# Second attention: each query tile's two maps scaled and added in two column halves; in the last layer, a low part read from PSUM and a norm bias made by pointer scalars

## The chip, the core and the metric

One core of a Trainium2 chip runs the whole program. The metric is device time in microseconds from one execution, the median of three runs. The engines are PE (TensorE, matrix products and transposes), DVE (VectorE), ACT (ScalarE), POOL (GpSimd) and SP (which issues DMAs). Each runs its own list of instructions in order and waits on semaphores that others raise. PE writes only to PSUM, which has eight banks here; POOL can't reach PSUM.

## What is computed

A block of four layers with residuals: attention of 16 heads, a mixture of experts, a second attention that subtracts one softmax map from another, and a gated layer with 4-bit quantization. The change lies in the last two (the shapes for x are 4 x 1024 x 128):

```python
attn = jax.nn.softmax(A1, axis=-1) - lam * jax.nn.softmax(A2, axis=-1)   # 8 heads
O = jnp.einsum('bhqk,bhkd->bhqd', attn, V)
rms = jnp.sqrt(jnp.mean(O * O, axis=-1, keepdims=True) + EPS)
...
x = x + _L1_attn_ref(_layernorm(x), ...)
x = x + _L1_ffn_ref(_layernorm(x), w_gate, w_up, w_down)
# _L1_ffn_ref: q(h) @ q(w_down).T, h = silu(q(x) @ q(w_gate).T) * (q(x) @ q(w_up).T), q = blockwise 4-bit
```

## The kernel before

A planner in plain Python (`plan_all`) writes one list of steps for all engines. Each engine walks through the list and emits its share of each step, so the list sets the order on every engine. `SIGNALS` says how often each step raises which semaphore; `at(name, step, i=k)` is the value after the k-th raise of a step, and `READ` says who frees a PSUM bank.

**The second attention** works on 256 query tiles of 128 rows (`NTAU`; 4 samples, 8 heads, 8 tiles each), one per slot of the loop over `n`. In a slot, per map `s` of the two: PE makes the scores of 128 x 1024 in six matmuls (`score`, L1798); DVE takes the negative row maxima (c_nm, L1376); ACT writes the exponentials and their row sums (`exponent`, L908, into the tile c_P of map s). Then `combine` joins the maps: DVE makes two factors per row (c_rr, L1383 and L1388); POOL multiplies the second map by its factor (L2046) and adds it to the first (L2048). It stands in the slot after the tile's scores. Three slots after the scores PE turns the joined map in two halves of four 128 x 128 blocks (`turn`, L1809); ACT writes a rounded copy (c_DT, L919) and DVE the rest, the low part (`low`, L1401); PE multiplies both with x (`pv`, L1825, into bank 6, copied out as c_Yh on ACT and c_Yl on DVE, L1409) and with the head's folded matrix (`output`, L1835). Every second slot PE makes the next head's left side (`c_project`, L1781), whose low part c_Tl is made on POOL (L2041). Banks 4, 5 and 7 are a ring for turns, outputs and the last layer's products.

**The last layer** is woven in, one pair of token tiles j per 16 slots. `norm1` takes statistics on DVE and a power on POOL (L2073); `norm2` makes the bias -mean/std on DVE (d_nb, L1508), and ACT writes the normed rows. Then come nine small steps of quantization, `xq` and, for the hidden row of the pair before, `hq`: maxima (L1463), scale (L1471), reciprocal (L1473), product (d_tn, L1475), two DVE steps (L1478, L1480), the snaps i = 6 and 7 on POOL (d_tn, L1099), and the product with the scale (L1485, d_x or d_h). `d_turn_x` turns d_x on PE; ACT writes the rounded copy d_xh (L981) and, in full, d_xl_f (L982); `d_turn_low` subtracts (L1514). The place that matters below is where the snaps of `hq` of one pair and `norm2` of the next stand beside two combines. The last query tile (n = 255) has its halves shared between DVE and POOL. The layer norm of the next sample is made in the same loop in three of the stretches.

Of the kernel before, what the change touches and what calls it, by code (L numbers as in the profile page):

```python
# [14 lines left out]
B, T, C = 4, 1024, 128  # L15
# [10 lines left out]
NTAU = B * 64  # L26
# [57 lines left out]
class Tally:  # L84
# [15 lines left out]
    def at(self, name, *step, i=None):  # L100

        return name, self.value[name, step] - (0 if i is None else self.by[name, step] - i)
# [44 lines left out]
def snapped(on_dve):  # L147
# [51 lines left out]
    "c_project_low": {"c_Tl": 1},  # L199
    "score": {"c_S": 1, "c_nm": 1},  # L200
    "exponent": {"c_ex": 1},
    "combine": lambda n: {"c_cc": 2, "c_D": 2, "c_Dd": 2 if n == NTAU - 1 else 0},
    "turn": {"c_tr": 1, "c_dh": 1},
    "low": {"c_dl": 1},
    "pv": lambda p, part: {"c_pv": 1, "c_yh": 1, "c_yl": 1} if part == 3 else {},
# [7 lines left out]
    "turn_weights_low": {"d_wtl": 1},  # L213
    "turn_down": {"d_h_pe": 1, "d_hT": 2},
    "norm1": {"d_ln": 5, "d_lnp": 1},
    "norm2": {"d_ln": 1, "d_xn": 2},
    "xq": lambda j, i: ON_POOL(i),
    "d_turn_x": {"d_x_pe": 1, "d_xh": 2},
    "d_turn_low": {"d_xl": 1},
    "gate": {"d_gu": 1, "d_sg": 1},  # L220
    "gate_factor": {"d_g": 1},
# [40 lines left out]
    "pv": lambda p, part: [("c_yl", "pv", p, 3)],  # L262
    "turn_weights": lambda k: [("d_wth", "turn_weights", k)],
    "turn_down": lambda: [("d_hT", "turn_down")],
    "d_turn_x": lambda j: [("d_xh", "d_turn_x", j)],
    "gate": lambda *a: [("d_g", "gate_factor", *a)],
    "up": lambda *a: [("d_h", "up", *a)],
    "d_turn_h": lambda *a: [("d_hT", "d_turn_h", *a)],
# [260 lines left out]
def memory(nc, io):  # L529

    m = Ctx()
# [13 lines left out]
    def plain(t):  # L545
        name, shape, offset = where[t.name]
        return nc.alloc_sbuf_tensor_at(name + "_f", shape, F32, offset=offset)
# [168 lines left out]
def scalar_engine(e, w, v, m):  # L716
    at, P = v.at, m.P8

    def bank(*step):
        return P[:, v.plan.bank[step], :]  # L720
# [253 lines left out]

    def d_turn_x(j):
        ps = bank("d_turn_x", j)
        hi, full = [t[:, :, :].rearrange("p i q -> p (i q)") for t in (m.fxh, m.fxf)]
        w.wait_ge(*at("d_x_pe", "d_turn_x", j))
        if j:
            w.wait_ge(*at("d_gu", "up", j - 1, 1))  # L980
        e.activation(hi, ps[:, 0:256], ACT.Copy).then_inc(m.S["d_xh"])  # L981
        e.activation(full, ps[:, 0:256], ACT.Copy).then_inc(m.S["d_xh"])  # L982

    def tanh(ps, i):
        e.activation(m.h[:, i, :], ps[:, 0:NF], ACT.Tanh, scale=0.5).then_inc(m.S["d_sg"])
# [20 lines left out]
    def l_gate(i):  # L1006
# [7 lines left out]
                 c_project=c_project, exponent=exponent, turn=turn, pv=pv, output=output, weigh=weigh,  # L1014
                 norm2=norm2, turn_weights=turn_weights,
                 turn_down=turn_down, d_turn_x=d_turn_x, gate=gate, d_turn_h=d_turn_h, l_turn_x=l_turn_x,
                 l_gate=l_gate)
    for kind, *a in v.plan.steps:
# [83 lines left out]
def vector_engine(e, w, v, m):  # L1102
    at, P = v.at, m.P8
# [400 lines left out]
    def norm2(j):  # L1504
        w.wait_ge(*at("d_lnp", "norm1", j))
        if j:
            w.wait_ge(*at("d_xn", "norm2", j - 1))
        e.scalar_tensor_tensor(out=m.fnb[:, :], in0=m.fmv[:, :, 0], scalar=-1.0, in1=m.fvr[:, 1, :], op0=ALU.mult,  # L1508
                               op1=ALU.mult).then_inc(m.S["d_ln"])

    def d_turn_low(j):
        hi, lo, full = [t[:, :, :].rearrange("p i q -> p (i q)") for t in (m.fxh, m.fxl, m.fxf)]
        w.wait_ge(*at("d_xh", "d_turn_x", j))
        e.tensor_tensor(lo, full, hi.bitcast(F32), ALU.subtract).then_inc(m.S["d_xl"])  # L1514

    def double_silu(ps, i):
        e.scalar_tensor_tensor(out=m.h[:, i, :], in0=m.h[:, i, :], scalar=1.0, in1=ps[:, 0:NF], op0=ALU.add,
# [53 lines left out]
    def l_down(i):  # L1571
# [8 lines left out]
                 small_exp=small_exp, scale=scale, fold=fold, c_turn_low=c_turn_low, keep_x=keep_x, score=score,  # L1580
                 combine=combine, low=low, pv=pv, factor=factor, add=add, turn_weights_low=turn_weights_low,
                 norm1=norm1, norm2=norm2, d_turn_low=d_turn_low, gate_factor=gate_factor, up=up, d_down=d_down,
                 l_norm=l_norm, l_turn_x=l_turn_x, l_silu=l_silu, l_times=l_times, l_down=l_down)
    e.memset(m.mh[:, :], -0.5).then_inc(m.S["mh"])
# [7 lines left out]
def tensor_engine(e, w, v, m):  # L1592
    at, P, ident = v.at, m.P8, m.ident

    def bank(*step):

        for t in v.freed(*step):
            w.wait_ge(*t)
        return P[:, v.plan.bank[step], :]
# [201 lines left out]
    def turn(n, half):  # L1801
        ps = bank("turn", n, half)
        if n == NTAU - 1:
            w.wait_ge(*at("c_D" if half else "c_Dd", "combine", n))
        else:
            w.wait_ge(*at("c_D", "combine", n))
        for i in range(4):
            kt = 4 * half + i
            tt = e.transpose(ps[:, 128 * i:128 * i + 128], m.P1[0][n % 4][:, 128 * kt:128 * kt + 128], ident)  # L1809
        tt.then_inc(m.S["c_tr"])  # L1810
# [103 lines left out]
    def l_down(i):  # L1914
# [5 lines left out]
                 divide=divide, turn_o=turn_o, out_project=out_project, m_turn_x=m_turn_x, route=route, spread=spread,  # L1920
                 item=item, down=down, finish=finish, small2=small2, fold=fold, c_turn_x=c_turn_x,
                 c_project=c_project, score=score, turn=turn, pv=pv, output=output, turn_weights=turn_weights,
                 turn_down=turn_down, d_turn_x=d_turn_x, gate=gate, up=up, d_turn_h=d_turn_h, d_down=d_down,
                 l_turn_x=l_turn_x, l_gate=l_gate, l_up=l_up, l_down=l_down)
# [6 lines left out]
def gpsimd_engine(e, w, v, m):  # L1931
    at = v.at
# [108 lines left out]
        e.tensor_tensor(lo, full, hi.bitcast(F32), ALU.subtract).then_inc(m.S["c_Tl"])  # L2041

    def combine(n):
        p0, p1 = [m.P1[s][n % 4][:, T // 2 if n == NTAU - 1 else 0:T] for s in range(2)]
        w.wait_ge(*at("c_cc", "combine", n))
        e.tensor_scalar(p1, p1, m.rr[:, n % 4, 1:2], 0.0, ALU.mult, ALU.add).then_inc(m.S["c_D"])  # L2046
        w.wait_ge(*at("c_D", "combine", n, i=1))
        e.tensor_tensor(p0, p0, p1, ALU.add).then_inc(m.S["c_D"])  # L2048

    def factor(u, first, end):  # L2050
        F, r = m.ff[u % 2], slice(first, end)
# [23 lines left out]
    def l_norm():  # L2075
        for i in range(2):
# [118 lines left out]
def build(nc, io, out):  # L2195
    with ExitStack() as ctx:
        v = Tally(plan_all(), SIGNALS, READ)
        m = memory(nc, io)
        m.P8 = ctx.enter_context(nc.psum_tensor("P", [128, 8, 512], F32))
        names = ["id", "mh", "a_w", "b_w", *[f"x{b}" for b in range(B + 1)], *v.end]  # L2200
        m.S = {n: ctx.enter_context(nc.semaphore(n)) for n in dict.fromkeys(names)}
        block = ctx.enter_context(nc.Block())
        block.sync(lambda e: sync_engine(e, Once(e, m.S), v, m, io, out))
        block.scalar(lambda e: scalar_engine(e, Once(e, m.S), v, m))
        block.vector(lambda e: vector_engine(e, Once(e, m.S), v, m))
        block.gpsimd(lambda e: gpsimd_engine(e, Once(e, m.S), v, m))
        block.tensor(lambda e: tensor_engine(e, Once(e, m.S), v, m))
# [66 lines left out]
```

## Time and profile before

| | us |
|---|---|
| runs | 2936.09, 2948.23, 2939.10 |
| median | 2939.1 |
| the profiled execution, its time | 2946.47 |
| its span, first to last instruction | 2944.7 |
| of it, loop of the second attention and the end | from about 1208 |

The profile is of one execution. A row of a timeline gives the start in us from the span's start, the length in us, engine, line, operation, out<-in, and in brackets the idle time of that engine just before and what ended it. Lengths of one engine overlap a little, since an instruction's end is seen when its result has landed. Windows give each engine's busy time in a stretch.

### The profile page before, as it was taken

To read this page: it belongs to the slowest core of one execution; us is meant where nothing else is said; L and a number is where in the kernel's file an instruction comes from. 1 tells how busy PE (TensorE), PEld (TensorE's weight loads), DVE (VectorE), ACT (ScalarE), POOL (GpSimd) and SP (SyncE) were. 2 spreads that over 40 slices of the span, in tenths; PEclk is the share of its full clock that TensorE was granted. 3 is DMA by queue.
4 is the path that set the end of the run, shared out by engine and by line. 5 is a ranking of instruction groups with operands and counts; after the bars stand their busy time and mean duration, and the time that the engine had idled before them with its cause. 6 is when DMAs were issued, how large, how long until landed. Compare 5 with 4: busy or idle time off the path is not lost.

```text
span 2944.7 us, 46590 instructions
## 1 busy us (share of the span) xinstructions
PE 2752.8 (93%) x16447; PEld 2032.8 (69%) x16447; DVE 2317.6 (79%) x4143; ACT 2126.2 (72%) x4692; POOL 1801.3 (61%) x1357
## 2 busy tenths in 40 slices
PE   6999999999899999999999999999999999999996
PEld 3333333333347777788888888888888888888885
DVE  8888888888937877789788777777777778777876
ACT  2677777777766555677877777777777787777773
POOL 3442524332015555677788777788778787777773
PEclk8899999999989999999999999999999999999997
DMA  1000000000022111000000000000000000000000
GB/s 41 7 7 7 12 7 7 7 7 2 2 76 75 48 48 58 8 1 1 1 1 3 3 1 3 3 1 3 3 1 3 3 1 3 3 1 3 3 3 6
DMA packets 25689, 34.83 MB, mean 12 GB/s; under 512 B 4136, under 2 KB 14952, under 8 KB 25456
## 3 DMA queue, kind: packets, MB, share of 16 engines
q1 hardware_dynamic: 25456, 31.85, 3.4%
q8 instruction: 131, 2.15, 0.3%
q14 instruction: 102, 0.84, 0.1%
HBM read 29.08 MB, written 2.23 MB: 11 GB/s over the span
## 4 chain that ended last, share of the span: by engine, by line
PE 67%; DVE 15%; ACT 8%; issue 6%; POOL 5%; DMA 0%; DVEq 0%; POOLq 0%; ACTq 0%
PE P L1798 18%; PE P L1666 9%; PE P L1825 8%; PE P L1809 6%; PE P L1651 5%; PE P L1727 5%; PE P L1639 4%; ACT a_PT L784 4%; DVE c_nm L1376 4%; DVE c_DT L1401 3%; PE P L1781 3%; PE P L1738 2%; PE P L1835 2%; PE P L1629 2%; POOL d_tn L1099 2%
## 5 line engine op out<-in xcount | busy, mean ns | idle before, releaser
L1376 DVE TENSOR_REDUCE c_nm<-P 128x1 f32<-128x1024 f32 x512 | 624.4, 1220 | 303.9 <-PE P L1798 301.9
L908 ACT ACTIVATE c_P<-P,c_nm 128x1024 f32<-128x1024 f32 x512 | 573.0, 1119 | 251.8 <-DVE c_nm L1376 247.5
L1221 DVE TENSOR_REDUCE a_mx<-P 128x1 f32<-128x512 f32 x1024 | 640.2, 683 | 99.5 <-PE P L1639 95.4
L784 ACT ACTIVATE a_PT<-P 128x512 f32<-128x512 f32 x1024 | 537.1, 603 | 165.4 <-PE P L1651 165.2
L2048 POOL TENSOR_TENSOR c_P<-c_P,c_P 128x1024 f32<-128x1024 f32 (+1 forms) x256 | 623.0, 2434 | 21.3
L2046 POOL TENSOR_SCALAR c_P<-c_P,c_rr 128x1024 f32<-128x1024 f32 (+1 forms) x256 | 300.9, 1176 | 338.4 <-DVE c_rr L1388 338.4
L1825 PE MATMUL P<-c_DT,c_xkh 128*128 128x256 f32 x2048 | 451.7, 283 | 24.7 <-DVE c_Yl L1409 23.0
L1651 PE MATMUL P<-a_Qs,a_Ks 32*128 32x512 f32 x1024 | 344.2, 493 | 59.6 <-ACT a_PT L784 53.2
L1825 PEld LDWEIGHTS P<-c_DT,c_xkh 128*128 128x128 f32 x2048 | 350.2, 189 | 37.0 <-DVE c_Yl L1409 29.2
L1798 PE MATMUL P<-c_xth,c_Th 128*128 128x512 f32 x1024 | 365.1, 437 | 2.8 <-ACT c_P L908 2.8
L1401 DVE TENSOR_TENSOR c_DT<-P,c_DT 128x512 fp32r<-128x512 f32 x512 | 348.4, 681 | 9.0 <-ACT c_DT L919 8.8
L1809 PE MATMUL P<-ident,c_P 128*128 128x128 f32 x2048 | 313.8, 276 | 37.2 <-DVE c_DT L1401 37.1
L1798 PE MATMUL P<-c_xtl,c_Th 128*128 128x512 f32 x1024 | 322.9, 397 | 0.0
L1798 PE MATMUL P<-c_xth,c_Tl 128*128 128x512 f32 x1024 | 319.9, 393 | 0.0
L919 ACT ACTIVATE c_DT<-P 128x512 fp32r<-128x512 f32 x512 | 305.9, 597 | 2.2 <-PE P L1809 1.9
L1639 PEld LDWEIGHTS P<-a_Ks,a_Qs 32*128 32x128 f32 x1024 | 128.6, 190 | 248.6 <-DVE a_mx L1221 193.5
L1639 PE MATMUL P<-a_Ks,a_Qs 32*128 32x512 f32 x1024 | 284.7, 494 | 11.5 <-DVE a_Qs L1213 5.4
L2034 POOL TENSOR_TENSOR b_sg<-b_sg,b_cwB 128x512 f32<-128x512 f32 x128 | 176.3, 1380 | 193.0 <-ACT b_sg L826 192.8
L1825 PE MATMUL P<-c_DT,c_xkl 128*128 128x256 f32 x1024 | 288.2, 281 | 0.0
L1666 PE MATMUL P<-a_PT,a_Vp 128*32 128x512 f32 x2048 | 282.6, 624 | 0.0
L1809 PEld LDWEIGHTS P<-ident,c_P 128*128 128x128 f32 x2048 | 233.3, 140 | 58.8 <-DVE c_DT L1401 58.2
L1651 PEld LDWEIGHTS P<-a_Qs,a_Ks 32*128 32x128 f32 x1024 | 134.7, 187 | 167.4 <-ACT a_PT L784 140.7
(245 smaller groups left out, 5393.6 us busy)
## 6 DMA issues: line engine op xcount, KB each, us to landing
b_cwB<-cw_scratch SPq DMA_DIRECT2D x64, 256.0 KB, 5.0
c_stg<-in_cw SPq DMA_DIRECT2D x8, 640.0 KB, 4.0
a_Qs<-a_mT SPq DMA_DIRECT2D x256, 2.0 KB
b_stg<-in_moe SPq DMA_DIRECT2D x9, 384.0 KB, 3.0
out<-xres SPq DMA_DIRECT2D x15, 128.0 KB, 1.8
xres<-in_x SPq DMA_DIRECT2D x3, 512.0 KB, 7.6
xres<-in_x SPq DMA_DIRECT2D x2, 256.0 KB, 3.0
a_hTl_f<-in_wqk SPq DMA_DIRECT2D x1, 512.0 KB, 3.6
```

The source lines that it names most:

```text
L784: e.activation(m.PT[j][hs % 4][:, :], bank("scores", u, hs, j), ACT.Exp, scale=SCALE).then_inc(m.S["a_exp"])
L908: e.activation(m.P1[s][n % 4][:, :], P[:, k:k + 2, :].rearrange("p c k -> p (c k)"), ACT.Exp, bias=m.nm[:, n % 4, s:s + 1], accum_out=m.sm ...
L1221: e.tensor_reduce(m.mx2[u % 2][:, t // 4, j, t % 4, half:half + 1], bank("maxima", u, t, j, half), AX, ALU.max).then_inc(m.S["a_max_dve"])
L1376: e.tensor_reduce(m.nm[:, n % 4, s:s + 1], P[:, k:k + 2, :].rearrange("p c k -> p (c k)"), AX, ALU.max, negate=True).then_inc(m.S["c_nm"])
L1401: e.tensor_tensor(lo, bank("turn", n, half).rearrange("p (t q) -> p t q", t=4), hi.bitcast(F32), ALU.subtract).then_inc(m.S["c_dl"])
L1639: e.matmul(ps, m.Qs[u % 3][r, 128 * t:128 * t + 128], m.Ks[u % 3][r, 512 * half:512 * half + 512], start=True, stop=True).then_inc(m.S["a_ ...
L1651: e.matmul(ps, m.Ks[u % 3][r, 128 * kt:128 * kt + 128], m.Qs[u % 3][r, 512 * c:512 * c + 512], start=True, stop=True).then_inc(m.S["a_st"])
L1666: tt = e.matmul(O[32 * j:32 * j + 32, :], m.Vp[b % 2][:, at_v:at_v + 32], m.PT[j][hs % 4][:, :], start=(kt == 0), stop=(kt == 7))
L1798: tt = e.matmul(ps[:, c, :], a[:, s, qs], x[:, 512 * c:512 * c + 512], start=(i == 0), stop=(i == 2))
L1809: tt = e.transpose(ps[:, 128 * i:128 * i + 128], m.P1[0][n % 4][:, 128 * kt:128 * kt + 128], ident)
L1825: tt = e.matmul(P[:, 6, 0:256], x[:, 128 * kt:128 * kt + 128], m.DT[p % 2][l][:, kt, :], start=(kt == 0 and j == 0), stop=(kt, j) == (7, 2))
L2048: e.tensor_tensor(p0, p0, p1, ALU.add).then_inc(m.S["c_D"])
```

## The change

1. `combine` on POOL works on columns 0 to 511 and then on 512 to 1023: scale, add, scale, add. It raises c_D four times instead of twice; `turn` of half 0 waits for the second raise, of half 1 for the fourth. The last query tile stays as it was.
2. `d_turn_x` on ACT writes only the rounded copy. `d_turn_low` on DVE subtracts it from the PSUM bank itself, with an added wait on `up` of the pair before, and it is now this step that frees the bank.
3. `norm2` on DVE makes the bias in two instructions of one column each, whose factor is a pointer scalar, in place of one instruction with two tensor inputs.

```diff
-    "combine": lambda n: {"c_cc": 2, "c_D": 2, "c_Dd": 2 if n == NTAU - 1 else 0},
+    "combine": lambda n: {"c_cc": 2, "c_D": 4, "c_Dd": 0} if n < NTAU - 1 else {"c_cc": 2, "c_D": 2, "c_Dd": 2},
...
-    "d_turn_x": lambda j: [("d_xh", "d_turn_x", j)],
+    "d_turn_x": lambda j: [("d_xl", "d_turn_low", j)],
...
         e.activation(hi, ps[:, 0:256], ACT.Copy).then_inc(m.S["d_xh"])
-        e.activation(full, ps[:, 0:256], ACT.Copy).then_inc(m.S["d_xh"])
...
-        e.scalar_tensor_tensor(out=m.fnb[:, :], in0=m.fmv[:, :, 0], scalar=-1.0, in1=m.fvr[:, 1, :], op0=ALU.mult,
-                               op1=ALU.mult).then_inc(m.S["d_ln"])
+        for i in range(2):
+            e.tensor_scalar(m.fnb[:, i:i + 1], m.fmv[:, i, 0:1], m.fvr[:, 1, i:i + 1], -1.0, ALU.mult,
+                            ALU.mult).then_inc(m.S["d_ln"])
...
         w.wait_ge(*at("d_xh", "d_turn_x", j))
-        e.tensor_tensor(lo, full, hi.bitcast(F32), ALU.subtract).then_inc(m.S["d_xl"])
+        if j:
+            w.wait_ge(*at("d_gu", "up", j - 1, 1))
+        e.tensor_tensor(lo, bank("d_turn_x", j)[:, 0:256], hi.bitcast(F32), ALU.subtract).then_inc(m.S["d_xl"])
...
-            w.wait_ge(*at("c_D", "combine", n))
+            w.wait_ge(*at("c_D", "combine", n, i=2 * half + 2))
...
-        p0, p1 = [m.P1[s][n % 4][:, T // 2 if n == NTAU - 1 else 0:T] for s in range(2)]
         w.wait_ge(*at("c_cc", "combine", n))
-        e.tensor_scalar(p1, p1, m.rr[:, n % 4, 1:2], 0.0, ALU.mult, ALU.add).then_inc(m.S["c_D"])
-        w.wait_ge(*at("c_D", "combine", n, i=1))
-        e.tensor_tensor(p0, p0, p1, ALU.add).then_inc(m.S["c_D"])
+        for i, half in enumerate((0, 1) if n < NTAU - 1 else (1,)):
+            p0, p1 = [m.P1[s][n % 4][:, T // 2 * half:T // 2 * half + T // 2] for s in range(2)]
+            e.tensor_scalar(p1, p1, m.rr[:, n % 4, 1:2], 0.0, ALU.mult, ALU.add).then_inc(m.S["c_D"])
+            w.wait_ge(*at("c_D", "combine", n, i=2 * i + 1))
+            e.tensor_tensor(p0, p0, p1, ALU.add).then_inc(m.S["c_D"])
```

How it moves instructions, first on POOL, at the place where two combines stand around the snaps of a hidden row. The operations are the scaling and the sum of c_P, the snaps d_tn, and c_Tl. Before:

```order
L2046 TENSOR_SCALAR c_P_0_184<-c_P_0_184,c_rr 128x1024
L2048 TENSOR_TENSOR c_P_0_180<-c_P_0_180,c_P_0_184 128x1024
L1099 TENSOR_TENSOR d_tn<-d_tn,d_tc 128x704 x2
L2046 TENSOR_SCALAR c_P_1_187<-c_P_1_187,c_rr 128x1024
L2048 TENSOR_TENSOR c_P_1_181<-c_P_1_181,c_P_1_187 128x1024
L2041 TENSOR_TENSOR c_Tl_192<-c_Tl_f,c_Th_191 128x512
```

After:

```order
L2049 TENSOR_SCALAR c_P_0_184<-c_P_0_184,c_rr 128x512
L2051 TENSOR_TENSOR c_P_0_180<-c_P_0_180,c_P_0_184 128x512
L2049 TENSOR_SCALAR c_P_0_184<-c_P_0_184,c_rr 128x512
L2051 TENSOR_TENSOR c_P_0_180<-c_P_0_180,c_P_0_184 128x512
L1098 TENSOR_TENSOR d_tn<-d_tn,d_tc 128x704 x2
L2049 TENSOR_SCALAR c_P_1_187<-c_P_1_187,c_rr 128x512
L2051 TENSOR_TENSOR c_P_1_181<-c_P_1_181,c_P_1_187 128x512
L2049 TENSOR_SCALAR c_P_1_187<-c_P_1_187,c_rr 128x512
L2051 TENSOR_TENSOR c_P_1_181<-c_P_1_181,c_P_1_187 128x512
L2043 TENSOR_TENSOR c_Tl_192<-c_Tl_f,c_Th_191 128x512
```

The two snaps and c_Tl keep their place in the row; ahead of each stand four instructions of 512 columns instead of two of 1024.

On DVE, at the norm of the last layer in the same stretch: the low part of a turned half (c_DT), the bias (d_nb), the row maxima of the next map (c_nm). Before:

```order
L1401 TENSOR_TENSOR c_DT_1_198<-P,c_DT_1_197 128x4x128
L1508 SCALAR_TENSOR_TENSOR d_nb<-d_mv,d_vr 128x2
L1376 TENSOR_REDUCE c_nm<-P 128x1
L1401 TENSOR_TENSOR c_DT_1_198<-P,c_DT_1_197 128x4x128
L1383 RECIPROCAL c_rr<-c_sm_162 128x1
```

After:

```order
L1400 TENSOR_TENSOR c_DT_1_198<-P,c_DT_1_197 128x4x128
L1508 TENSOR_SCALAR d_nb<-d_mv,d_vr 128x1 x2
L1375 TENSOR_REDUCE c_nm<-P 128x1
L1400 TENSOR_TENSOR c_DT_1_198<-P,c_DT_1_197 128x4x128
L1382 RECIPROCAL c_rr<-c_sm_162 128x1
```

The bias stands where it stood, as two instructions in place of one.

## Rows read from the trace of the kernel before

**Rows 1.** The page of the profile: the span, and each engine's busy time.

```profile
span 2944.7 us, 46590 instructions
...
PE 2752.8 (93%) x16447; PEld 2032.8 (69%) x16447; DVE 2317.6 (79%) x4143; ACT 2126.2 (72%) x4692; POOL 1801.3 (61%) x1357
```

**Rows 2.** Two stretches as windows: start:end, length, busy us (instructions), PE clock, DMA.

```profile
1586.00:1693.00 107.00, 101.79 (x640) 90.52 (x639) 82.22 (x136) 81.87 (x196) 82.71 (x55) 1.00 0.01 2
1907.00:2014.00 107.00, 102.03 (x646) 91.01 (x645) 85.27 (x151) 82.71 (x198) 90.87 (x64) 1.00 0.01 2
```

**Rows 3.** Waits of PE from 1210 to 2880 us: total us, times, longest.

```profile
PE P L1809 <- DVE c_DT L1401: 35.3, 98, 1.3
PE P L1825 <- DVE c_Yl L1409: 22.6, 13, 1.8
```

**Rows 4.** Timeline of PE, 1583 to 1616 us: start, length, then the idle time before.

```profile
1590.31 0.38 PE L1781 MATMUL P<-c_xth,c_mh 128*128 128x256 f32 x1 [0.20 <-DVE c_DT L1401]
...
1598.64 0.39 PE L1825 MATMUL P<-c_DT,c_xkh 128*128 128x256 f32 x1 [1.73 <-DVE c_Yl L1409]
...
1603.99 0.65 PE L1809 MATMUL P<-ident,c_P 128*128 128x128 f32 x4 [0.91 <-DVE c_DT L1401]
...
1611.19 0.66 PE L1809 MATMUL P<-ident,c_P 128*128 128x128 f32 x4 [0.35 <-DVE c_DT L1401]
```

**Rows 5.** Timeline of POOL, the same stretch.

```profile
1586.81 1.33 POOL L2046 TENSOR_SCALAR c_P<-c_P,c_rr 128x1024 f32<-128x1024 f32 x1 [1.46 <-DVE c_rr L1388]
1588.23 2.55 POOL L2048 TENSOR_TENSOR c_P<-c_P,c_P 128x1024 f32<-128x1024 f32 x1
1590.74 3.49 POOL L1099 TENSOR_TENSOR d_tn<-d_tn,d_tc 128x704 f32<-128x704 f32 x2
1594.21 1.12 POOL L2046 TENSOR_SCALAR c_P<-c_P,c_rr 128x1024 f32<-128x1024 f32 x1
1595.41 2.88 POOL L2048 TENSOR_TENSOR c_P<-c_P,c_P 128x1024 f32<-128x1024 f32 x1
1598.26 1.28 POOL L2041 TENSOR_TENSOR c_Tl<-c_Tl_f,c_Th 128x512 fp32r<-128x512 f32 x1
...
1603.22 2.38 POOL L2048 TENSOR_TENSOR c_P<-c_P,c_P 128x1024 f32<-128x1024 f32 x1
```

**Rows 6.** Timeline of DVE, the same stretch.

```profile
1587.18 1.34 DVE L1480 TENSOR_SCALAR d_tc<-d_tc 128x704 f32<-128x704 f32 x1
...
1590.17 0.62 DVE L1508 SCALAR_TENSOR_TENSOR d_nb<-d_mv,d_vr 128x2 f32<-128x2 f32 x1
...
1594.36 1.72 DVE L1485 TENSOR_TENSOR d_h<-d_tn,d_sc 128x704 f32<-128x704 f32 x1 [1.06 <-POOL d_tn L1099]
...
1598.50 1.07 DVE L1471 TENSOR_SCALAR d_sc<-d_mx 128x16 f32<-128x16 f32 x1
...
1603.26 0.67 DVE L1401 TENSOR_TENSOR c_DT<-P,c_DT 128x512 fp32r<-128x512 f32 x1
1603.86 2.02 DVE L1475 SCALAR_TENSOR_TENSOR d_tn<-d_x,d_mx 128x256 f32<-128x256 f32 x1
...
1609.31 1.23 DVE L1376 TENSOR_REDUCE c_nm<-P 128x1 f32<-128x1024 f32 x1 [0.67 <-PE P L1798]
```

**Rows 7.** POOL's groups by form: shapes, count, busy us, mean ns.

```profile
L1999 POOL TENSOR_SCALAR a_th<-a_th,a_msk 128x512 f32<-128x512 f32 x61 | 42.1, 691 | 6.0
L2005 POOL TENSOR_TENSOR a_Qs<-a_th,a_tq 128x512 fp32r<-128x512 f32 x31 | 39.5, 1274 | 2.6
```

**Rows 8.** Single lines: count, shortest/median/longest ns, first and last start.

```profile
L1388 DVE TENSOR_SCALAR c_rr<-c_sm,c_nlam,c_rr x256: 271/273/277, 1208.4 to 2892.8; 128x1 f32<-128x1 f32 x128
...
L1409 DVE TENSOR_TENSOR c_Yl<-P,c_Yh x128: 407/424/427, 1235.3 to 2909.8; 128x256 fp32r<-128x256 f32 x128
...
L1514 DVE TENSOR_TENSOR d_xl<-d_xl_f,d_xh x15: 425/490/907, 1411.3 to 2899.4; 128x256 fp32r<-128x256 f32 x15
...
L982 ACT ACTIVATE d_xl_f<-P x15: 378/407/418, 1409.7 to 2898.9; 128x256 f32<-128x256 f32 x15
```

More of the change, by code:

```diff
@@ L215 @@
     "norm1": {"d_ln": 5, "d_lnp": 1},
-    "norm2": {"d_ln": 1, "d_xn": 2},
+    "norm2": {"d_ln": 2, "d_xn": 2},
     "xq": lambda j, i: ON_POOL(i),
-    "d_turn_x": {"d_x_pe": 1, "d_xh": 2},
+    "d_turn_x": {"d_x_pe": 1, "d_xh": 1},
     "d_turn_low": {"d_xl": 1},
@@ L691, in memory @@
     assert top <= c_small, top
-    m.fxf, m.fwf = plain(m.fxl), plain(m.fwl)
+    m.fwf = plain(m.fwl)
     return m
@@ L976, in d_turn_x @@
         ps = bank("d_turn_x", j)
-        hi, full = [t[:, :, :].rearrange("p i q -> p (i q)") for t in (m.fxh, m.fxf)]
+        hi = m.fxh[:, :, :].rearrange("p i q -> p (i q)")
         w.wait_ge(*at("d_x_pe", "d_turn_x", j))
@@ L1507, in norm2 @@
             w.wait_ge(*at("d_xn", "norm2", j - 1))
-        e.scalar_tensor_tensor(out=m.fnb[:, :], in0=m.fmv[:, :, 0], scalar=-1.0, in1=m.fvr[:, 1, :], op0=ALU.mult,
-                               op1=ALU.mult).then_inc(m.S["d_ln"])
+        for i in range(2):
+            e.tensor_scalar(m.fnb[:, i:i + 1], m.fmv[:, i, 0:1], m.fvr[:, 1, i:i + 1], -1.0, ALU.mult,
+                            ALU.mult).then_inc(m.S["d_ln"])
     def d_turn_low(j):
-        hi, lo, full = [t[:, :, :].rearrange("p i q -> p (i q)") for t in (m.fxh, m.fxl, m.fxf)]
+        hi, lo = [t[:, :, :].rearrange("p i q -> p (i q)") for t in (m.fxh, m.fxl)]
         w.wait_ge(*at("d_xh", "d_turn_x", j))
-        e.tensor_tensor(lo, full, hi.bitcast(F32), ALU.subtract).then_inc(m.S["d_xl"])
+        if j:
+            w.wait_ge(*at("d_gu", "up", j - 1, 1))
+        e.tensor_tensor(lo, bank("d_turn_x", j)[:, 0:256], hi.bitcast(F32), ALU.subtract).then_inc(m.S["d_xl"])
     def double_silu(ps, i):
```

## Prediction

> **What bounds the kernel now.** I read the page first, then the windows of the second attention, PE's waits there, and last the timelines of one stretch of 16 query tiles. The page gives a span of 2944.7 us in which PE is busy for 93% and POOL for 61% [rows 1]. The change touches only the second attention and the last layer, which is woven into it. There PE is busy for 101.8 of 107 us at full clock, while DVE, ACT and POOL are all near 82; where the next block's norm is made, POOL reaches 90.9 [rows 2]. So PE is the bound, with about 5 us of gaps in each stretch of 16 tiles. Where are the gaps? In PE's waits all large ones end with DVE: 35.3 us on the low part of the turned map and 22.6 us on c_Yl; no row of PE waits for POOL [rows 3]. So nobody stands at the door of `combine`, the step that is split. Its first sum (POOL, from 1603.22, 2.38 us long) ends at 1605.60, and PE turns this tile at 1611.19, 5.6 us later [rows 4, 5].
>
> The gaps fall at the same place in each stretch: 1.73 us before 1598.64 and 0.91 us before 1603.99, then small ones of 0.2 to 0.5 us [rows 4]. What leads there is seen from POOL and DVE side by side. POOL runs without a gap from 1586.81 to 1599.54: the two instructions of a combine, two snaps of the last layer's hidden row (d_tn, 3.49 us), a second combine, one c_Tl [rows 5]. DVE waits 1.06 us for the second snap, then does d_h (L1485), and all of DVE's work for PE queues behind it: PE starts again 2.56 us after d_h's end [rows 4, 6].
>
> The timelines also show that DVE and POOL stop each other. DVE's d_tn (L1475, 256 columns) starts at 1603.86 and ends at 1605.88, 0.28 us after POOL's sum; DVE's d_h starts at 1594.36, in POOL's scaling, which ends at 1595.33, and ends 0.75 us after that, at 1596.08; the POOL sum that was issued at 1595.41 takes 2.88 us instead of 2.38, as it waits for d_h; L1471, on 16 columns, starts at 1598.50 and ends at 1599.57, when POOL's c_Tl ends [rows 5, 6]. So a DVE instruction of that kind waits for the end of the POOL instruction in progress, and goes before POOL's next one. This is the mechanism by which shorter POOL instructions can help.
>
> **The split of the combine.** Removed per tile: one scaling and one sum over 1024 columns, undisturbed 1.12 and 2.38 us, with 0.08 us between them [rows 5]; in all 3.58 us. Added: two pairs over 512 columns. The nearest rows are a scaling with a pointer scalar, 0.69 us, and a sum, 1.27 us [rows 7]. The tile then takes 2 x (0.69 + 0.08 + 1.27) = 4.08 us, 0.50 more, on 255 tiles. The last tile is as before. Bounds for the extra: 0 (work scales with columns) and 0.9 (each half sum costs 0.2 more than that row); I take 0.5. On the whole POOL has room: 16 x 0.5 = 8 us more makes 91 of 107, and 99 in the three fullest stretches [rows 2]. The first half of a map is ready 1.5 us earlier (after 2.04 instead of 3.58 us), which pays nothing, since PE comes 5.6 us later. The c_Tl behind it comes later too; the scores that need it start at about the gap of 1603.99, 4.4 us after its end at 1599.54 [rows 4, 5]. Cover: both.
>
> What counts is the piece of POOL's queue ahead of the second snap. **First half of the place.** Now the scaling is issued at 1586.81, takes 1.33 us, and DVE's L1480 waits for it until 1588.52 [rows 5, 6]. With halves: scaling done at about 1587.72 (0.69 plus the same 0.21 of delay); L1480 then needs 0.4 and ends at 1588.14, 0.38 earlier; the sum waits for it and ends at 1589.4; second scaling to 1590.1; second sum to 1591.4; two snaps of together 3.49 end at 1594.85 instead of 1594.23. So the second snap is 0.6 late. **Second half.** Call the end of the second snap S. Now d_h must wait for the scaling of 1.12 and ends at S + 1.85. With halves it waits for 0.69 and ends at S' + 1.44, with S' = S + 0.62: S + 2.06, so 0.2 late. PE's gap of 1.73 becomes 1.9. Then: first sum to S' + 2.65, second scaling to S' + 3.35, second sum from S' + 3.43 to S' + 4.70. L1471 starts 2.42 us after d_h's end [rows 6], at S' + 3.86, inside this second sum, and ends with it: S' + 4.73 = S + 5.35. Now it ends at 1599.57 = S + 5.34. So DVE is again where it was, and DVE is what PE waits for at 1603.99: the low part at 1603.26 [rows 4, 6]. The longer first gap is given back in the second. Sum for this place: 0.0 us, with 0.4 us of doubt on either side (POOL's extra per pair between 0 and 0.9, two pairs on the way), times 14 stretches (15 tile pairs go through the last layer inside the loop, and the first finds no hidden row of an earlier one there): 0 ± 11 us, taken as 12.
>
> **Third place**, d_tn and the two L1478/L1480 behind it. Now d_tn loses 1.5 us to the sum, and the two after it none, because POOL does a c_ff then. With halves d_tn ends at 1604.3 instead of 1605.88; but the other two each meet a new POOL half, and I get 1606.6 for their end instead of 1606.5. DVE has 0.67 us to spare before 1609.31 [rows 6], so either way PE sees nothing: 0.
>
> **The norm's bias.** One instruction on 128x2 with two tensor inputs, 0.62 us, which ends with POOL's sum (1588.23 + 2.55 = 1590.78) [rows 5, 6], goes; two with a pointer scalar on 128x1 come, 0.27 us each in a row of that form that never varied (271 to 277 ns in 256) [rows 8]. They cost some 0.45 us together, at most 0.54. Gain 0.1 to 0.2 us on DVE, but DVE waits 1.06 us for the snap right behind [rows 6], so it is worth 0. If both waited for POOL the cost would be 0.
>
> **The low part from PSUM.** Removed: 15 ACT copies of 0.41 us. The subtraction now reads PSUM; such a one took 407 to 427 ns in 128 cases, where the old one took 425 to 907 [rows 8]. DVE gains 0.07 (median) to 0.5 us each; neither is where PE's gaps are made. The added wait on `up` of the tile pair before is long past. The bank goes free with DVE's read instead of ACT's second one; the ring of three banks comes back to it only with the third take after it. Worth 0; if the cover fails, 0.4 us x 15 = 6.
>
> On that last row a rule of the Trainium skill bears (GPSIMD Engine Reference, Specifications): GpSimd's SBUF interface is shared with VectorE, and collisions come with DVE instructions that have two SBUF inputs or use two ports. By that rule the subtraction from PSUM never waits for POOL, and DVE gains 15 x 0.15 = 2 us on the mean by it; by the old row's 0.49 it would gain 1 us. The trace agrees so far: all 128 c_Yl are undisturbed.
>
> **Sum.** Period place 0, third place 0, bias 0, low part 0; for the end of the loop, where PE waits for DVE almost all the time and the snaps come late once more, +1 us. On the profiled execution 2946.5 + 1 = 2947.5. That execution lies 7.4 us above the median of 2939.1; on the median I forecast **2940 us**.
>
> **Rivals.** *Gain:* the locks shrink more than POOL grows. This holds if a half costs POOL less than rows 7 say, so that L1471 no longer waits: 1.07 x 14 = 15 us [rows 6], 2925. For it: DVE's waits for POOL are real and long. Against: behind the combine stands c_Tl, the next POOL instruction to wait for. *Loss:* L1471 comes after the second sum's end and so waits for c_Tl, another 1.28 us [rows 5], and PE's second gap grows by it: 14 x 1.28 = 18 us, 2958. It decides at 0.84 us (S' + 4.70 against S' + 3.86); one d_h that is delayed by one more half instruction does it. *Not what it says:* somebody waits for the first half after all, and the split frees him; no row shows one, so it would be the forecast's time.
>
> **Chances.** Forecast, with its ± 12: 0.80, of which a little at either rim. Gain 0.09, loss 0.11. A measurement of this kernel tells about 0.5% (14.7 us) from no change, so faster 0.09, same 0.80, slower 0.11. The range is the forecast's own, 2928 to 2952.
>
> **What would show it.** Right: L2048's successors at 1.27 us and L2046's at 0.69; the second snap 0.6 us later after the norm's bias; d_h (L1485) near 1.3 instead of 1.72 us; PE's gap before the pv matmul near 1.9 and the next one near 0.7. Wrong: PE waiting for POOL in a turn, an L1471 that ends with c_Tl, or stretches of 16 tiles that are no longer 107 us long. If halves cost 1.6 us each, as they would if DVE disturbed every one, POOL fills the three full stretches and the sum is off.

## The result and the profile after

The changed kernel took 2956.8 us (median of 20 runs) against 2948.1 us for the kernel before beside it (20 runs): ratio 1.004, with a 95% interval of 1.0028 to 1.0052. The medians lie 8.7 us apart, and the ratio, taken over all runs, is worth 12 us. The change is thus 9 to 12 us slower: inside what was called "no change" (0.5%), but clear of zero, and 2956.8 lies above the predicted range. The page of the changed kernel, and the two windows of [rows 2]:

```profile
span 2950.7 us, 47341 instructions
...
PE 2754.4 (93%) x16447; PEld 2038.9 (69%) x16447; DVE 2292.1 (78%) x4158; ACT 2123.8 (72%) x4677; POOL 1906.6 (65%) x1867
```

```profile
1586.00:1693.00 107.00, 101.40 (x637) 90.14 (x635) 80.43 (x135) 80.92 (x194) 88.62 (x87) 1.00 0.01 2
1907.00:2014.00 107.00, 101.12 (x643) 90.64 (x643) 83.61 (x154) 82.75 (x197) 96.08 (x96) 1.00 0.01 2
```

Against [rows 1, 2], POOL has 105 us more work, 5 to 6 us in each 107, DVE has 25 us less, and PE's busy time over the whole span is nearly the same. In the 14 stretches of 16 tiles (from the first d_nb to the last, first before, then after) it isn't:

```profile
1379.53:2873.89 1494.36, 1431.92 (x8975) 1277.44 (x8975) 1152.36 (x1939) 1145.93 (x2731) 1177.15 (x796) 1.00 0.01 2
```

```profile
1373.77:2878.15 1504.38, 1438.65 (x8975) 1284.31 (x8975) 1132.72 (x1953) 1143.14 (x2717) 1269.45 (x1245) 0.99 0.01 2
```

For the same 8975 instructions PE is busy for 6.7 us more, and it is idle for 3.3 us more (65.7 against 62.4). The place with the snaps looks as the prediction drew it. POOL, start and length:

```profile
1582.27 0.89 POOL L2049 TENSOR_SCALAR c_P<-c_P,c_rr 128x512 f32<-128x512 f32 x1 [1.39 <-DVE c_rr L1387]
1583.25 1.44 POOL L2051 TENSOR_TENSOR c_P<-c_P,c_P 128x512 f32<-128x512 f32 x1
1584.66 0.69 POOL L2049 TENSOR_SCALAR c_P<-c_P,c_rr 128x512 f32<-128x512 f32 x1
1585.44 1.29 POOL L2051 TENSOR_TENSOR c_P<-c_P,c_P 128x512 f32<-128x512 f32 x1
1586.68 3.50 POOL L1098 TENSOR_TENSOR d_tn<-d_tn,d_tc 128x704 f32<-128x704 f32 x2
1590.16 0.69 POOL L2049 TENSOR_SCALAR c_P<-c_P,c_rr 128x512 f32<-128x512 f32 x1
```

The snaps end 7.91 us after the first scaling began, and 7.42 us in [rows 5]: 0.49 us late. DVE in the same stretch:

```profile
1582.64 0.91 DVE L1479 TENSOR_SCALAR d_tc<-d_tc 128x704 f32<-128x704 f32 x1
...
1585.19 0.32 DVE L1508 TENSOR_SCALAR d_nb<-d_mv,d_vr 128x1 f32<-128x1 f32 x2
...
1590.31 1.28 DVE L1484 TENSOR_TENSOR d_h<-d_tn,d_sc 128x704 f32<-128x704 f32 x1 [2.04 <-POOL d_tn L1098]
...
1594.01 0.76 DVE L1470 TENSOR_SCALAR d_sc<-d_mx 128x16 f32<-128x16 f32 x1
```

The product d_h takes 1.28 us instead of 1.72, and the scale d_sc 0.76 instead of 1.07 [rows 6], but DVE waits 2.04 us for the snap instead of 1.06. PE's waits from 1210 to 2880 us (total, times, longest), to be laid beside [rows 3]; the first block is of the kernel before, rows that were not shown there:

```profile
PE P L1781 <- DVE c_DT L1401: 3.1, 15, 0.3
PE P L1825 <- DVE c_xkl L1368: 1.7, 3, 0.6
```

```profile
PE P L1811 <- DVE c_DT L1400: 29.9, 97, 1.1
PE P L1827 <- DVE c_Yl L1408: 29.1, 13, 2.2
PE P L1783 <- DVE c_DT L1400: 4.5, 13, 0.7
...
PE P L1827 <- DVE c_xkl L1367: 3.2, 3, 1.1
```

The wait ahead of the pv matmul for c_Yl rose from 22.6 to 29.1 us, the one of the turns for the low part fell from 35.3 to 29.9. So part of the second gap of the place moved into the first: 1.73 and 0.91 us before [rows 4], 2.23 and 0.67 after. Behind the longer one this is seen on PE (timeline, start and length; first at one place, then 110 us later):

```profile
1484.73 0.58 PE L1827 MATMUL P<-c_DT,c_xkh 128*128 128x256 f32 x1 [2.25 <-DVE c_Yl L1408]
1485.11 0.42 PE L1827 MATMUL P<-c_DT,c_xkl 128*128 128x256 f32 x1
...
1594.15 0.38 PE L1827 MATMUL P<-c_DT,c_xkh 128*128 128x256 f32 x1 [2.23 <-DVE c_Yl L1408]
1594.38 0.28 PE L1827 MATMUL P<-c_DT,c_xkl 128*128 128x256 f32 x1
...
1599.20 0.66 PE L1811 MATMUL P<-ident,c_P 128*128 128x128 f32 x4 [0.67 <-DVE c_DT L1400]
```

The same matmuls, the same gap ahead of them, and 0.42 us instead of 0.28 for one. Windows of PE's granted clock (last but two column) ahead of the first place and in it:

```profile
1477.00:1481.50 4.50, 4.50 (x31) 4.15 (x31) 2.25 (x7) 4.09 (x11) 4.35 (x4) 1.00 0.00 0
1484.50:1487.50 3.00, 2.77 (x12) 2.67 (x13) 2.93 (x7) 1.73 (x4) 2.05 (x2) 0.50 0.00 0
```

PE was busy at full clock, then idle for 2.25 us, and came back at a granted clock of 0.50, the 1.2 GHz level. I call this a fall. In the 14 stretches of 16 tiles inside the loop there are 2 falls in the kernel before and 7 in the changed one. What one costs is read from neighbouring stretches (from one d_nb to the next): before, 107.1 us with a fall and 106.1 without; after, 107.6 and 106.4. So about 1.1 us (0.7 to 1.2 in these two kernels). All these are plain stretches, without a layer norm and without c_xkl; most others are up to 2 us longer in either kernel. Two sums result. Five falls more are some 5.5 us. And a stretch without a fall is 0.3 us longer (106.4 against 106.1), 4 us in 14. From the first combine to the end the traces differ by 12.1 us (1748.1 against 1736.0), as much as the ratio says: 10.0 us in the 14 stretches, 2 us outside them, most of it behind the last. (The spans differ by 6.0 only, since the profiled execution of after happened to be 6 us shorter ahead of the first combine, where nothing is changed.)

### The profile page after: what moved, and what is told of

Same layout as the page of the kernel before. It is cut to its first block, busy times and chain, and to the rows that moved or that the text cites. A ratio compares the mean times of both kernels' runs of the same rounds, so it can differ in the third digit from the quotient of the medians.

```text
span 2950.7 us, 47341 instructions
## 1 busy us (share of the span) xinstructions
PE 2754.4 (93%) x16447; PEld 2038.9 (69%) x16447; DVE 2292.1 (78%) x4158; ACT 2123.8 (72%) x4677; POOL 1906.6 (65%) x1867
## 3 DMA queue, kind: packets, MB, share of 16 engines
HBM read 29.08 MB, written 2.23 MB: 11 GB/s over the span
## 4 chain that ended last, share of the span: by engine, by line
PE 73%; DVE 14%; ACT 7%; issue 5%; POOL 2%; DMA 0%; DVEq 0%; POOLq 0%
PE P L1800 21%; PE P L1827 9%; PE P L1668 8%; PE P L1811 7%; PE P L1653 5%; PE P L1729 5%; PE P L1641 4%; DVE c_nm L1375 4%; ACT a_PT L784 4%; DVE c_DT L1400 3%; PE P L1783 3%; PE P L1837 2%; PE P L1740 2%; PE P L1631 2%; DVE a_mx L1220 1%
## 5 line engine op out<-in xcount | busy, mean ns | idle before, releaser
L2051 POOL TENSOR_TENSOR c_P<-c_P,c_P 128x512 f32<-128x512 f32 x511 | 668.8, 1309 | 42.6
L2049 POOL TENSOR_SCALAR c_P<-c_P,c_rr 128x512 f32<-128x512 f32 x511 | 370.7, 725 | 224.3 <-DVE c_rr L1387 224.2
```

## The experiments

I began with two theories. **Clock (C):** the split lengthens one gap of PE, and the clock behind it is the cost. **POOL (P):** each halved tile costs by its additional 0.5 us of POOL work, wherever it stands. A third (O), that the two small edits cost something, went with the first two runs. In all of them the reference is the kernel before, run beside them.

**One part alone, and the whole without it.** The first is the kernel before with edit 1 only (its lines with +), the second the changed kernel with edit 1 taken back (with -):

```diff
+        for i, half in enumerate((0, 1) if n < NTAU - 1 else (1,)):
+            p0, p1 = [m.P1[s][n % 4][:, T // 2 * half:T // 2 * half + T // 2] for s in range(2)]
...
-        for i, half in enumerate((0, 1) if n < NTAU - 1 else (1,)):
-            p0, p1 = [m.P1[s][n % 4][:, T // 2 * half:T // 2 * half + T // 2] for s in range(2)]
```

> Edit: the kernel before with the column halves of the combine alone; the low part and the bias stay as they were. Theory C (clock): in the changed kernel PE's gap ahead of the pv matmul, once in each stretch of 16 tiles, grew from 1.73 to 2.23 us, and PE's clock fell behind it in 7 of 14 stretches, against 2 of 14 before; each fall costs about 1.1 us of a stretch (107.6 against 106.4 us). The gap grew because POOL's two combines push the snaps and because PE no longer stops 0.2 us earlier. With the split alone the snaps are late by 0.5 us, the bias instruction (two tensor inputs) still waits for POOL: gap 1.9 to 2.2 us, 4 to 8 falls, +6 to +12 us. Theory P (POOL's queue): the 0.5 us more per tile cost the time directly, in the stretches with a layer norm above all, whatever the clock does: +10 to +12 us, with the same number of falls as before. Theory O (the two small edits cost it): 0 to +3 us here.

> Edit: the changed kernel with the combine whole again; low part from PSUM and bias by pointer scalars stay. Theory C: the snaps are where they were, PE comes up to 0.2 us earlier, gap 1.75 to 1.95 us, 2 to 5 falls of the clock: 0 to +4 us against the kernel before. Theory P: 0 to -2 us. Theory O: +9 to +12 us.

Measured: 1.0046 (1.0030 to 1.0063), 9 falls, gap 2.25 us; and 0.9999 (0.9982 to 1.0015), 1 fall, gap 1.73 us. The split carries all of it; bias and low part cost nothing and bring nothing that can be measured. With 9 falls and 14 us the first lies a little above what C had expected. One reason that C gives there is wrong: in most stretches of the changed kernel PE still waits 0.2 to 0.3 us at L1783, and the gap is 2.24 us all the same. Why it grew is said below.

**The gap without the split.** The kernel before, with two short instructions on DVE behind d_h, whose results nobody uses, in 14 stretches; POOL is untouched. In the second, each reads 256 columns instead of 128.

```diff
+            if kind == "xq" and 0 < j < NJ - 1:
+                for k in range(2):
+                    e.bn_stats(m.fst[:, k, :], m.fx[:, k, :])
             e.tensor_reduce(mx, blk(src), AX, ALU.max, apply_absolute_value=True).then_inc(s)
```

> Edit: the kernel before, POOL untouched, with two more statistics instructions (0.24 us each, result unused) on DVE behind the product that ends the hidden row's quantization, in 14 stretches. They lengthen PE's gap ahead of the pv matmul from 1.73 to about 2.2 us. Theory C: 6 to 10 falls instead of 2, each 1.1 us, plus what DVE is later at the second gap (0.48 x 14 = 7 us): +10 to +16 us. Theory P: the clock has no part, +7 us at most from DVE's own 0.48, and falls as before (2 or 3).

> Edit: the kernel before, POOL untouched, with two more statistics instructions over 256 columns (about 0.37 us each, result unused) on DVE behind d_h, in 14 stretches. PE's gap becomes about 2.4 to 2.5 us. Theory C: the falls in the loop grow with the gap, after 0 at 1.3 us, 1 or 2 at 1.73, 5 at 2.13, 7 to 9 at 2.24: 9 to 14 here, +9 to +18 us. If only DVE's own time counts: 5 falls or fewer, and 14 x 0.25 = 3.5 us above the run with the two shorter ones.

Measured: 1.0031 (1.0013 to 1.0049), gap 2.13 us, 5 falls; and 1.0039 (1.0023 to 1.0056), gap 2.39 us, 8 falls. Both have fewer falls than C had expected, and the first costs less (9 us). It is still the cleanest case for C. DVE's additional work is absorbed a little later, since L1471 and L1475 then wait less for POOL, and stretches without a fall take 106.1 us as before. The 14 stretches of the first:

```profile
1377.31:2875.43 1498.12, 1436.05 (x8975) 1280.98 (x8974) 1148.99 (x1965) 1147.72 (x2731) 1178.64 (x796) 0.99 0.01 2
```

PE is idle for 62.1 us, no more than before (62.4), and busy for 4.1 us more with the same instructions. The stretches are 3.7 us longer in sum; the five with a fall are 0.8 to 1.4 us longer than the same ones before, and three more falls at 1.1 us are 3.3. So longer gaps, with no change on POOL, make the clock fall and the kernel slower.

**Whole only ahead of the snaps.** The changed kernel, where tile 12 of each 16 (the one ahead of the snaps) is combined in one piece; 240 of 255 keep their halves.

```diff
+def cuts(n):
+    h = T // 2
+    return [(h, T)] if n == NTAU - 1 else [(0, T)] if n % 16 == 12 else [(0, h), (h, T)]
...
-        for i, half in enumerate((0, 1) if n < NTAU - 1 else (1,)):
+        for i, (first, end) in enumerate(cuts(n)):
```

> Edit: the changed kernel, but every sixteenth tile, the one whose combine stands ahead of the hidden row's snaps on POOL, is combined whole. 240 of 255 tiles are still halved, so POOL keeps nearly all of its extra work. Theory C: the snaps come 0.1 to 0.5 us earlier, PE's gap is 1.7 to 2.0 us, falls 2 to 5: +3 to +7 us against the kernel before, 5 to 8 less than the changed kernel. Theory P: the extra work is nearly the same, +10 to +12 us.

Measured: 2942.9 us, 0.9986 (0.9969 to 1.0003), gap 1.29 us, no fall, 105.9 us for a stretch. The whole loss is gone with some 15 tiles, and more than C had expected (a gap of 1.7 us, 2 falls, +3 us at best): the half behind the snaps still shortens d_h by 0.4 us. I took P for dead here, which was too early.

**The gap moved instead of shortened.** d_h half a slot later on DVE, behind c_Yl, in the changed kernel, in the kernel before, and in the one that is whole ahead of the snaps:

```diff
-        out += [(n + at[8] + a if at[8:] else n + 8 + i / 2, ("hq", j, i)) for i, a in enumerate(QUANT_H)]
+        late_h = (*QUANT_H[:8], 3.5) if j < NJ - 3 else QUANT_H
+        out += [(n + at[8] + a if at[8:] else n + 8 + i / 2, ("hq", j, i)) for i, a in enumerate(late_h)]
```

> Edit: the changed kernel, halves everywhere, with one step of the last layer half a slot later on DVE: the product that ends the hidden row's quantization (d_h), which waited for the late snaps, now stands behind the low part c_Yl that frees PE. 13 of the 15 pairs. Theory C (clock behind the gap): PE's gap of 2.24 us goes or becomes small (under 1 us), no fall of the clock in the loop; time 14 to 26 us below the changed kernel, thus 3 to 15 us below the kernel before. Theory P (POOL's extra half microsecond per tile costs time as such): POOL's work and order are unchanged, so the time stays near the changed kernel's, at most 5 us below it.

> Edit: the kernel before with the same step moved. Theory C: gap of 1.73 us goes, the 2 falls too: 8 to 20 us below the kernel before, and within 5 us of the changed kernel with the same move, since what was left between them was the clock. Theory P: the changed kernel with the move stays 10 to 12 us above this one.

> Edit: the kernel with every sixteenth tile whole (240 of 255 halved) with the same step moved. With the gap gone there is nothing left for the whole tile to save. Theory C: within 3 us of the changed kernel with the move. A theory by which halves shorten DVE's waits for POOL elsewhere: 3 to 8 us below the kernel before with the move.

Measured: 1.0044 (1.0031 to 1.0058), 8 falls; 1.0108 (1.0085 to 1.0130), 12 falls; 0.9976 (0.9960 to 0.9991), 2 falls. The wait for c_Yl went as meant, but I had expected the gap to vanish, and it stands now one step later, ahead of a matmul that needs the next low part: 2.04, 1.97 and 1.65 us in most stretches, and 2.4 to 2.6 (first) or 2.0 (third) in the three with a layer norm. All three expectations failed in their numbers: the first is 13 us above the kernel before, the second 32 us above it, and the third 20 us below the first. With the gaps as they came out, the first and the third go with C. The two falls of the third stand behind its gaps of 2.02 and 2.06 us; behind its ten gaps of 1.62 to 1.68 us there is none. The second doesn't fit in size: with 1.97 us it has more falls than kernels with 2.1 to 2.4, and nine of the 12 last twice as long. It alone has a second gap, mostly of 0.9 us, that ends only 2.4 us after the first one (5.3 us in the kernel before); whether that is the reason no run tests. The single gap's length is thus not all that counts; what else does in this kernel stays open.

**Where the other 0.5 us per stretch come from.** Two runs to test P again: whole combines on both tiles around the snaps (12 and 13), and halves on tile 13 only.

```diff
-    return [(h, T)] if n == NTAU - 1 else [(0, T)] if n % 16 == 12 else [(0, h), (h, T)]
+    return [(h, T)] if n == NTAU - 1 else [(0, T)] if n % 16 in (12, 13) else [(0, h), (h, T)]
+    return [(h, T)] if n == NTAU - 1 else [(0, T)] if n % 16 != 13 else [(0, h), (h, T)]
```

> The changed kernel with whole combines on the two tiles of each 16 that stand around the two snaps in POOL's queue (numbers 12 and 13); the other tiles keep their halves, about 224 of 255. Theory C (one single gap of PE, ahead of the pv matmul that waits for c_Yl, decides how often the granted clock falls): d_h again waits for a whole scaling of 1.12 us, so the gap is 1.73 us as in the kernel before, 1 to 3 falls in 14 stretches, stretches without a fall of 106.1 us, and 2944 to 2948 us, ratio 0.999 to 1.001. Theory P (more POOL work costs time wherever it stands): 224 of 255 tiles still have halves, so most of the loss stays, 2953 to 2956 us, ratio 1.003.

> Halves on a single tile of each 16 only, the one behind the two snaps (number 13); about 16 tiles of 255 are halved. Theory C: the snaps are as early as in the kernel before and d_h waits for a half scaling of 0.69 us only, so the gap ahead of the pv matmul is 1.3 us, no fall in the loop, stretches without a fall of 105.9 us, 2940 to 2944 us, ratio 0.998 to 0.9995, the same as with 240 halved tiles. Theory P: the 224 halves less are worth what the change cost, so this is 10 us below the kernel with 240 halved tiles, near 2933 us.

Measured: 2953.1 us, 1.0020 (1.0002 to 1.0037), gap 1.73 us, 1 fall, 106.6 us for a stretch; and 2935.2 us, 0.9966 (0.9946 to 0.9987), gap 1.3 us, no fall, 105.4 us. The first lies between what C and P had expected, the second near P's value. Both contradict C alone: 224 halves cost 0.5 us per stretch in either pair (106.6 against 106.1, 105.9 against 105.4) with no change in falls. PE's waits, first with 240 halved tiles, then with one in 16:

```profile
PE P L1788 <- DVE c_DT L1405: 10.5, 16, 0.8
PE P L1832 <- DVE c_xkl L1372: 3.3, 3, 1.1
```

```profile
PE P L1788 <- DVE c_DT L1405: 3.0, 14, 0.3
PE P L1832 <- DVE c_xkl L1372: 1.7, 3, 0.6
```

The wait for c_Yl is the same (16.8 and 17.0 us). These two differ, by 7.5 and 1.6 us, and they are not at the snaps. What DVE does ahead of the first is the variance d_vr. DVE, then POOL, with 240 halved tiles:

```profile
1798.26 0.71 DVE L1506 TENSOR_SCALAR d_vr<-d_mv 128x2 f32<-128x2 f32 x1
```

```profile
1797.66 1.29 POOL L2048 TENSOR_TENSOR c_Tl<-c_Tl_f,c_Th 128x512 fp32r<-128x512 f32 x1
```

An instruction over 128x2 that takes 0.71 us ends at 1798.97, and POOL's c_Tl ends at 1798.95. It is the lock of the prediction at a place where the prediction didn't look. The single line over the loop, length of the shortest, median and longest in ns, before and after:

```profile
L1502 DVE TENSOR_SCALAR d_vr<-d_mv x15: 169/192/599, 1375.2 to 2868.1; 128x2 f32<-128x2 f32 x15
```

```profile
L1501 DVE TENSOR_SCALAR d_vr<-d_mv x15: 292/692/724, 1369.7 to 2872.3; 128x2 f32<-128x2 f32 x15
```

Before, c_Tl ends just as d_vr comes; with halves in the tile ahead of it, it begins 4.63 us after the tile's scaling instead of 4.11, and d_vr ends with it. c_xkl, between two SBUF tensors, waits in the same way behind the c_Tl of tile 3 (1.22 us instead of 0.70). This became theory **L**: a half costs only where a c_Tl that comes later for it stops such a DVE instruction on PE's path.

**Whole at the locks.** Whole on tiles 3, 11 and 12 of each 16, halves on the other 13 of 16:

```diff
+    return [(h, T)] if n == NTAU - 1 else [(0, T)] if n % 16 in (3, 11, 12) else [(0, h), (h, T)]
```

> The changed kernel with whole combines on tiles 3, 11 and 12 of each 16; the other 13 of 16 keep their halves. Tile 12 is the one ahead of the snaps; behind tiles 11 and 3 stands a c_Tl for whose end a DVE instruction between two SBUF tensors (the variance d_vr, c_xkl) was seen to wait. Theory L (a half costs time only where the c_Tl behind it, 0.5 us later, holds such a DVE instruction on PE's path): as with one halved tile in 16, c_xkl's gap back from 1.10 to 0.58 us, the gap at the norm's place back from 0.69 to 0.2, stretches without a fall 105.4 us, no falls, about 2935 us, ratio 0.9965. Theory P (each halved tile costs 0.03 us wherever it stands): 192 tiles more are halved than with one in 16, 6 us, so 2941 us, stretches of 105.8 us.

Measured: 2936.8 us, 0.9961 (0.9946 to 0.9977), gap 1.3 us, no fall in the loop, 105.4 us for a stretch. DVE and POOL at the norm, and PE's waits:

```profile
1692.63 0.20 DVE L1506 TENSOR_SCALAR d_vr<-d_mv 128x2 f32<-128x2 f32 x1
```

```profile
1691.50 1.30 POOL L2048 TENSOR_TENSOR c_Tl<-c_Tl_f,c_Th 128x512 fp32r<-128x512 f32 x1
```

```profile
PE P L1788 <- DVE c_DT L1405: 4.8, 16, 0.7
...
PE P L1832 <- DVE c_xkl L1372: 1.7, 3, 0.6
```

L is borne out and P is dead this time: 192 halves more than with one in 16 cost nothing in a plain stretch. POOL's sheer work (88.45 us busy in the window from 1586 to 1693) doesn't matter there. In the three stretches with a layer norm they cost 0.5 to 0.7 us each, partly made up for elsewhere; the 14 stretches take 1483.9 us against 1482.9. There DVE's c_xtl (128x512, two tensors in SBUF) meets a half sum of POOL, and not a c_Tl. Whole at the locks, then tile 13 only:

```profile
L1364 DVE TENSOR_TENSOR c_xtl<-c_xtl_f,c_xth x8: 678/684/1785, 1174.2 to 2426.0; 128x512 fp32r<-128x512 f32 x8
```

```profile
L1364 DVE TENSOR_TENSOR c_xtl<-c_xtl_f,c_xth x8: 677/678/683, 1173.2 to 2423.2; 128x512 fp32r<-128x512 f32 x8
```

So L in its words is too narrow: a half can also stop such an instruction itself.

**Both gains together.** Halves on tile 13 only, and d_h half a slot later.

> Halves on tile 13 of each 16 only, and d_h half a slot later on DVE, behind c_Yl: the two edits that each brought time so far, together. If they add up, the move is worth the 5 us that it was worth on the kernel with 240 halved tiles (2942.85 to 2937.67), so about 2930 us, ratio 0.995, stretches of 104.8 us without a fall. By theory C the largest gap is then near 1.65 us and there are 0 to 3 falls in the loop; a gap of over 2 us would bring five or more of them, and take the gain back.

Measured: 2940.5 us, 0.9976 (0.9956 to 0.9995), gap 2.09 us, 5 falls, 105.2 us for a stretch. They don't add up: a stretch is only 0.2 us shorter, and the gap, longer than the 1.65 us that I had counted on, brings the falls.

| kernel | gap | falls of 14 | stretch without a fall | ratio |
|---|---|---|---|---|
| whole ahead of the snaps; 13 only; whole at the locks | 1.3 | 0, 0, 0 | 105.9; 105.4; 105.4 | 0.9986; 0.9966; 0.9961 |
| whole and late d_h | 1.65, three of 2.0 | 2, both behind 2.0 | 105.3 | 0.9976 |
| before; without the split; both whole | 1.73 | 2, 1, 1 | 106.1; 106.1; 106.6 | 1; 0.9999; 1.0020 |
| before and late d_h | 1.97 | 12 | | 1.0108 |
| after and late d_h; 13 only and late d_h | 2.04; 2.09 | 8, 5 | 105.8; 105.2 | 1.0044; 0.9976 |
| before, DVE 0.5 us longer | 2.13 | 5 | 106.1 | 1.0031 |
| after; split alone | 2.24 | 7, 9 | 106.4; 106.4 | 1.0040; 1.0046 |
| before, DVE longer still | 2.39 | 8 | 106.1 | 1.0039 |

The gap is that of the plain stretches, and so is the time. Falls and gaps are from one profiled execution of each kernel, so that one or two falls more or less mean little; the ratios are from 6 to 20 runs.

The two best versions, halves on tile 13 only and whole at the locks, are faster than both kernels, by 0.3 to 0.4% against the one before.

## Why the prediction was wrong

Forecast was 2940 us, 1 us above the 2939.1 of three runs; measured were 2956.8. Of the 17 us between them 9 are no effect of the change: in 20 runs the kernel before has a median of 2948.1. The other 9 to 12 are, and the forecast had 1 us for them.

**The lock, and the place around the snaps: right.** Put forward was a scaling of 0.69 and a sum of 1.27 us (most are 0.69 and 1.28); snaps 0.6 us late (0.49); d_h near 1.3 us (1.28); the second gap near 0.7 (0.67). The first gap is 2.23 instead of 1.9. Counted from the start of the first scaling, d_h ends only 0.05 us later and PE's gap ends at 11.88 us instead of 11.83, but the gap begins at 9.65 instead of 10.10. The reason is the lock once more: DVE's step L1480 was held for less time (0.91 us instead of 1.34), so that DVE and PE behind it come 0.4 us earlier to the same late snap. The prediction had L1480 end 0.38 us earlier and didn't carry that over to PE. Over the whole place the forecast of 0.0 ± 0.4 us holds: PE is past the second gap 16.93 us after the first scaling began, instead of 17.18. The runs even split it: the half behind the snaps gives 0.7 us per stretch (106.1 to 105.4 with tile 13 alone), the half ahead of them takes 0.5 (105.9 to 106.4). The third place was right too, with d_tn at 0.48 us instead of 2.02, the two steps behind it longer, and PE's small gap of 0.35 us as before.

**The step that failed first: "Cover: both", for the c_Tl behind a combine.** I asked who needs c_Tl, found the scores 4.4 us away, and booked its delay at nothing. The question was also whom POOL stops while it works on it. I had just described that lock, and applied it only to the DVE instructions at the snaps and behind them. At tile 11 it costs 0.5 us in each stretch, at tile 3 another 0.5 in the three stretches with c_xkl; in the three with a layer norm a half sum that stops c_xtl comes on top. For a plain stretch the runs then give 106.1 - 0.7 + 0.5 + 0.5 = 106.4 us, and the changed kernel has 106.4.

**The second: "The longer first gap is given back in the second. Sum for this place: 0.0 us."** As time on the way through this place it is so. But two gaps of 1.73 and 0.91 us are not worth the same as 2.23 and 0.67, since behind the longer one PE's granted clock fell to 0.50 in 7 of 14 stretches instead of 2. The term was 0 and came to some 5.5 us, five falls more at 1.1 us. The trace of before had two such falls, at 1814 and 2565 us, each right behind the gap of 1.73, and I didn't look for them: a stretch of 107.1 us among ones of 106.1 shows them.

The Trainium skill says in TensorE: Matmul & The Clock Gate, A second HAM failure mode: psum-queue depth-cycling, that short idle times of PE between groups of matmuls can make its clock go back and forth, and that the price is paid in the throughput between the bursts. The traces agree in kind, with about 1.1 us for a fall; which gap does it here only the runs told.

**Bias, low part: right.** d_nb takes 197 to 208 ns in 30 cases, 0.32 us for the pair instead of 0.62, and d_xl 414 to 425 ns in 15; the kernel without the split is at 0.9999. In the same sense the rule that was weighed there (the Trainium skill, GPSIMD Engine Reference, Specifications) held for the subtraction from PSUM; and c_xkl, which has the two SBUF inputs of that rule, is among those that are stopped.

**The rivals.** That the loss was named with 2958 us, near the measured 2956.8, is luck: it stood for 18 us of loss, of which 9 to 12 took place, and its cause was wrong, since L1471 didn't wait for c_Tl (0.76 us long, 1.07 before). The gain did take place, L1471 and d_h both became shorter; it is what tile 13 alone shows, 0.9966, with 0.7 x 14 = 10 us instead of the 15 that were named, and the changed kernel spent it elsewhere.

## What to carry to other kernels

If a resource stops another engine per instruction, a piece of work that gets longer must be followed to all that queues behind it there, and for each of those one asks both who needs its result and whom it stops while it runs. Sum PE's gaps, but also list the longest: behind gaps of 2.1 us the clock fell in 5 stretches and behind gaps of 1.7 in 2, in two kernels with the same idle time of PE in sum. Work that shortens a lock also lets the engine behind it come earlier to the next wait, which then grows. A uniform split of a repeated step is best tried per position; here one position of 16 carried the gain and three the loss; the other twelve together cost 1 us in 14 stretches.

## What the runs showed of the hardware

- The granted clock of PE fell to 0.50 (1.2 GHz) for some 3 us, in nine of the 12 falls of one kernel and one of another for twice as long, behind single gaps of 1.7 to 2.6 us in stretches that otherwise ran at full clock. Behind gaps of 1.3 us it never did so in 39 places (13 in each of three kernels, since the first stretch has no such gap), nor in 10 places behind 1.65; behind 1.73 us in 4 of 39; behind 2.0 to 2.6 us in 44 of 81. The kernel with 1.97 us, where a second gap follows closely, stands apart with 12 of 13. The same gap, to 0.02 us, is followed by a fall in one stretch and not in the next. A fall costs 0.7 to 1.7 us, less than its length, since PE then has fewer waits behind it (the gap of 0.91 us is gone in both such stretches of the kernel before).
- DVE's d_vr over 128x2 elements takes 0.19 us or, behind a POOL instruction in progress, up to 0.72; c_xtl over 128x512 takes 0.68 or 1.79; those over 128x1 with a pointer scalar were never stopped (197 to 208 ns in 30 cases).
- On POOL a sum over 512 columns takes 1.28 us and one over 1024 takes 2.38, a scaling 0.69 and 1.12: two halves cost 0.44 us more than the whole, besides the gap between them.
